# Top-64 attention kernel: diagonals of reciprocals for the turned probabilities, the test for missed rows on GpSimd, and VectorE in ScalarE's place for the first value product of a step

## What is computed

```python
dots = jnp.concatenate([q @ mem_k.T, q @ k.T]) * scale       # 16 memory keys + 512 keys, 16 heads
dots = jnp.einsum('bhij,hk->bkij', dots, pre_proj)           # heads mixed
dots = jnp.where(causal, neg, dots)
vk   = lax.top_k(dots, 64)[0][..., -1:]                      # the 64th largest of each row
attn = softmax(jnp.where(dots < vk, neg, dots))
attn = jnp.einsum('bhij,hk->bkij', attn, post_proj)          # heads mixed again
out  = (attn @ v) @ Wo + bo
x = x + layernorm(out);  x = x + layernorm(ffn(layernorm(x)))
```

## Time and profile before

| | |
|---|---|
| median of 3 runs | 3364.86 us (3363.4 to 3366.53) |
| the profiled execution's own time | 3363.66 us |
| its span, first to last instruction | 3361.9 us |
| TensorE busy | 2675.5 us (80%) |
| VectorE busy | 2958.5 us (88%) |
| ScalarE busy | 2891.6 us (86%) |
| GpSimd busy | 1887.2 us (56%) |
| mean granted TensorE clock | 0.903 |

### The profile page before, as it was taken

How to read it: one execution, slowest core, us unless ns; L and a number is a source line. 1 busy time by engine, 2 the same in 40 slices (tenths; PEclk the granted TensorE clock), 3 DMA queues, 4 the chain that set the end, 5 groups by cost and what they waited for, 6 DMA issues and landing times. The chain is left out here.

```text
span 3361.9 us, 70684 instructions
## 1 busy us (share of the span) xinstructions
PE 2675.5 (80%) x13754; PEld 1771.9 (53%) x13754; DVE 2958.5 (88%) x12547; ACT 2891.6 (86%) x8666; POOL 1887.2 (56%) x3623
## 2 busy tenths in 40 slices
PE   7878888888877888888787867887788887888765
PEld 3455555555545555555555545555455555555543
DVE  4599999999989999999999989998999999998985
ACT  1699989898978989999898978989899898989972
POOL 3455566555655555566565546655565665555543
PEclk8989899898988998999999888989899899999977
DMA  1000000000000000000000000000000000000000
GB/s 44 7 2 2 5 8 5 9 2 5 8 5 9 2 9 5 5 9 5 8 2 11 2 5 8 3 11 2 5 8 5 9 2 11 2 5 9 2 8 4
DMA packets 31404, 22.66 MB, mean 7 GB/s; under 512 B 3201, under 2 KB 30338, under 8 KB 30722
## 3 DMA queue, kind: packets, MB, share of 16 engines
q1 hardware_dynamic: 30722, 16.03, 1.7%
HBM read 11.83 MB, written 4.19 MB: 5 GB/s over the span
## 5 line engine op out<-in xcount | busy, mean ns | idle before, releaser
L913 ACT ACTIVATE signs<-scores,state 128x528 int8<-128x528 f32 (+3 forms) x3072 | 1723.5, 574 | 74.7 <-DVE state L1146 74.2
L1347 POOL TENSOR_SCALAR probs<-probs,rinv 128x528 f32<-128x528 f32 (+3 forms) x1024 | 538.9, 545 | 1300.6 <-DVE rinv L1193 1300.6
L783 PE MATMUL t_bank<-ident,probs 128*128 128x128 f32 x2560 | 485.5, 334 | 601.9 <-POOL probs L1347 593.6
L1355 POOL TENSOR_TENSOR work<-scores,work 128x528 f32<-128x528 f32 (+3 forms) x1024 | 888.3, 900 | 11.6 <-DVE work L1073 11.6
L759 PE MATMUL s_bank<-xn,gT 128*128 128x512 f32 (+3 forms) x2048 | 761.8, 496 | 1.8 <-ACT gT L844 0.7
L783 PEld LDWEIGHTS t_bank<-ident,probs 128*128 128x128 f32 x2560 | 325.7, 164 | 708.6 <-issue 582.5
L770 PEld LDWEIGHTS y_bank<-u_all,probsT 128*128 128x128 f32 x5120 | 616.8, 194 | 109.4 <-issue 98.8
L770 PE MATMUL y_bank<-u_all,probsT 128*128 128x128 f32 x5120 | 625.4, 278 | 6.6 <-ACT probsT L924 6.5
L924 ACT COPY probsT<-t_bank 128x512 f32<-128x512 f32 (+1 forms) x768 | 400.5, 522 | 251.2 <-PE t_bank L783 247.6
L913 ACT ACTIVATION_READ_ACCUMULATOR signs<-scores,state 128x1 f32 x3072 | 614.7, 200 | 0.0
L1073 DVE TENSOR_SCALAR_CACHE_REDUCE work<-scores,state 128x528 f32<-128x528 f32 (+3 forms) x1024 | 531.1, 553 | 46.2 <-DVE state L1146 46.2
(11 more groups left out here) (156 smaller groups left out, 2984.0 us busy)
## 6 DMA issues: line engine op xcount, KB each, us to landing
xwork<-in_L_attn_x_dram SPq DMA_DIRECT2D x17, 256.0 KB, 2.8
xres<-in_L_attn_x_dram SPq DMA_DIRECT2D x16, 256.0 KB, 2.9
out_dram<-ybuf SPq DMA_DIRECT2D x16, 256.0 KB, 2.4
u_all<-in_L_attn_Wq_dram SPq DMA_DIRECT2D x1, 512.0 KB, 3.5
u_all<-in_L_attn_Wk_dram SPq DMA_DIRECT2D x1, 512.0 KB, 4.4
u_all<-in_L_attn_Wv_dram SPq DMA_DIRECT2D x1, 512.0 KB, 5.3
u_all<-in_L_attn_Wo_dram SPq DMA_DIRECT2D x1, 512.0 KB
expo<-in_L_ffn_w_gate_dram SPq DMA_DIRECT2D x1, 192.0 KB, 4.7
```

The costliest lines, as they stand in the source:

```text
L783: mm = nc.tensor.transpose(t_bank[q % 2][:, at:at + P], probs[:, h % 2, KEY_AT[t] + j * P:KEY_AT[t] + (j + 1) * P], ident[:, :])
L913: nc.scalar.activation(signs[:, k, AT[t]:AT[t] + ROW[t]], row(scores, ring(head_of(s, k + 1), RING), t), ACT.Sign, bias=guesses(s % STATES ...
L1347: nc.gpsimd.tensor_scalar(prb, prb, rinv[:, slot_p, t:t + 1], 1.0, ALU.mult, ALU.mult).then_inc(scaled, 1)
L1355: nc.gpsimd.tensor_tensor(wrk, row(scores, slot_k, t), wrk, ALU.subtract).then_inc(hidden, 1)
```

## The change

It has three parts.

1. **Diagonals.** GpSimd no longer scales `probs` in place. It makes four 128 x 128 tiles `diag[t] = ident * rinv[t]`, and TensorE replaces each transpose by an ordinary matmul with the diagonal as its right side, which turns and scales at once. `pmem` is then a product with `rinv` and no longer a copy. Ahead of the diagonals GpSimd also waits for `t_full`, the last turn of the head before.
2. **Missed rows and `between` on GpSimd.** `spread` and `missed` leave VectorE; GpSimd makes them behind `offset`, which gets two more columns per tile (`reach`) so that `spread` is a product of two of them. The sum over the tiles is taken where VectorE copies the flags. The first operation of the secant step, `between = ...`, leaves VectorE too and stands behind `missed` on GpSimd; VectorE waits for it (`between_ready`) ahead of the operation that uses it.
3. **First value product.** The `U` product at place 0 of a step (nine of 16 steps: s = 0, 1, 2, 3, 4, 5, 9, 10, 15) is copied out of PSUM by VectorE, at the end of its step, and no longer by ScalarE.

```diff
@@ TensorE, turn
-                        mm = nc.tensor.transpose(t_bank[q % 2][:, at:at + P],
-                                                 probs[:, h % 2, KEY_AT[t] + j * P:KEY_AT[t] + (j + 1) * P], ident[:, :])
+                        mm = nc.tensor.matmul(t_bank[q % 2][:, at:at + P],
+                                              lhsT=probs[:, h % 2, KEY_AT[t] + j * P:KEY_AT[t] + (j + 1) * P],
+                                              rhs=diag[:, t, :], start=True, stop=True, skip_group_check=True)
@@ ScalarE, take_extra
-                            take_values(kind, b, par, use[1])
+                            if place == 1:
+                                take_values(kind, b, par, use[1])
@@ VectorE, step
-                        v.tensor_copy(flags[:, :], flag_part).then_inc(flag_taken, 1)
+                        v.tensor_scalar(flags[:, 0:T], flag_part, 1.0, None, ALU.mult, ALU.add,
+                                        accum_out=flags[:, T:T + 1]).then_inc(flag_taken, 1)
...
-                    if checks:
-                        number = found[:, (s - 1) % 2, :]
-                        dve.wait_ge(found_ready, 4 * ge + 4)
-                        alone(dve)
-                        v.scalar_tensor_tensor(out=spread[:, :], in0=number, scalar=-2.0 * AIM, in1=number,
-                                               op0=ALU.add, op1=ALU.mult).then_inc(select_step, 1)
-                        dve.wait_ge(select_step, 1)
-                        at_least(dve, flag_full, ge)
-                        alone(dve)
-                        v.scalar_tensor_tensor(out=missed[:, 0:T], in0=spread[:, :], scalar=WINDOW ** 2 + 0.5 - AIM ** 2,
-                                               in1=active, op0=ALU.is_gt, op1=ALU.mult,
-                                               accum_out=missed[:, T:T + 1]).then_inc(bad_ready, 1)
...
-                        v.tensor_tensor(between[:, :, :], pair(past, S_T, -1), pair(last, S_OTHER, 0),
-                                        ALU.subtract).then_inc(guess_step, 1)
...
-                        dve.wait_ge(guess_step, 3)
+                        dve.wait_ge(guess_step, 2)
+                        dve.wait_ge(between_ready, g - 1)
+                        alone(dve)
                         v.scalar_tensor_tensor(out=between[:, :, :],
...
+                    use = extra(kind, s, 0)
+                    if use is not None and use[0] == "U":
+                        u = use[1]
+                        dve.wait_ge(misc_full, misc_index(kind, b, use) + 1)
+                        at_least(dve, pv_done, (b - 1) * H + 4 * (u // 4) + 4)
+                        alone(dve)
+                        v.tensor_copy(u_all[:, u % 4, 512 * (u // 4):512 * (u // 4 + 1)],
+                                      misc[misc_place(kind, par, use)][:, :]).then_inc(misc_free[misc_place(kind, par, use)], 1)
@@ GpSimd, step
-                        nc.gpsimd.tensor_tensor(offset[:, :, 0:9], ranks,
-                                                found[:, (s - 1) % 2, :].unsqueeze(2).to_broadcast([P, T, 9]),
+                        nc.gpsimd.tensor_tensor(offset[:, :, 0:11], ranks,
+                                                found[:, (s - 1) % 2, :].unsqueeze(2).to_broadcast([P, T, 11]),
                                                 ALU.add).then_inc(offset_ready, 1)
+                        ge = g - LAG_E
+                        pool.wait_ge(offset_ready, ge + 1)
+                        alone(pool)
+                        nc.gpsimd.tensor_tensor(spread[:, :], offset[:, :, 0:1].squeeze(2), offset[:, :, 1:2].squeeze(2),
+                                                ALU.mult).then_inc(spread_ready, 1)
+                        pool.wait_ge(spread_ready, ge + 1)
+                        at_least(pool, flag_full, ge)
+                        alone(pool)
+                        nc.gpsimd.tensor_scalar(missed[:, :], spread[:, :], 0.0, 1.0, ALU.is_gt, ALU.mult).then_inc(bad_ready, 1)
+                    if any(lagged(kind, s, k + 2) for k in range(GUESSES)):
+                        last, past = (s - 1) % STATES, (s - 2) % STATES
+                        at_least(pool, guess_ready, g - 2)
+                        at_least(pool, first_ready, g - 1 if lagged(kind, s, 2) else 0)
+                        alone(pool)
+                        nc.gpsimd.tensor_tensor(between[:, :, :], pair(past, S_T, -1), pair(last, S_OTHER, 0),
+                                                ALU.subtract).then_inc(between_ready, 1)
                     extras(kind, b, s)
...
                         at_least(pool, probs_ready, 4 * gp + 4)
+                        at_least(pool, t_full, 3 * gp)
                         alone(pool)
                         for t in SCORE_ORDER:
-                            prb = probs[:, slot_p, AT[t]:AT[t] + ROW[t]]
-                            nc.gpsimd.tensor_scalar(prb, prb, rinv[:, slot_p, t:t + 1], 1.0, ALU.mult,
+                            nc.gpsimd.tensor_scalar(diag[:, t, :], ident[:, :], rinv[:, slot_p, t:t + 1], 1.0, ALU.mult,
                                                     ALU.mult).then_inc(scaled, 1)
```

More of the change, by code:

```diff
@@ L324, in build @@
         centre = sb("centre", [P, P])
+        diag = sb("diag", [P, T, P])
         row_sum = sb("row_sum", [P, 2 * HC])
@@ L342, in build @@
         found = sb("found", [P, 2, T])
-        offset = sb("offset", [P, T, 10])
+        offset = sb("offset", [P, T, 12])
         spread = sb("spread", [P, T])
-        missed = sb("missed", [P, T + 1])
+        missed = sb("missed", [P, T])
         flags = sb("flags", [1, T + 1])
@@ L443, in build @@
         select_step = sem("select_step")
+        spread_ready = sem("spread_ready")
         bad_ready = sem("bad_ready")
+        between_ready = sem("between_ready")
         scaled = sem("scaled")
@@ L1053, in _ @@
             dve.wait_ge(state_set, 3)
-            nc.vector.tensor_copy(offset[:, :, 9:10].squeeze(2), cap)
+            nc.vector.tensor_copy(offset[:, :, 11:12].squeeze(2), cap)
             def batch(kind, b, par):
@@ L1088, in step @@
                         dve.wait_ge(offset_ready, gp + 1)
[L1089 to L1090 removed]
+                        dve.wait_ge(select_step, T)
+                        v.scalar_tensor_tensor(out=offset[:, :, 2:11], in0=offset[:, :, 2:11], scalar=0.0,
                                                in1=candidates(past), op0=ALU.is_equal,
                                                op1=ALU.mult).then_inc(select_step, 1)
[L1093 removed]
+                        dve.wait_ge(select_step, T + 1)
                         dve.sem_clear(select_step)
[L1095 removed]
+                        v.tensor_reduce(kth[:, bass.ds(slot_p, 1), :].squeeze(1), offset[:, :, 2:12], AX_X,
                                         ALU.add).then_inc(kth_ready, 1)
[L1098 to L1109 removed]
                     if moves:
@@ L1358, in step @@
                             pool.wait_ge(misc_full, misc_index(kind, b, ("PM", 1)) + 1)
-                        pool.wait_ge(scaled, 4 * gp + 4)
                         alone(pool)
-                        nc.gpsimd.tensor_copy(head_mem(pmem, head_of(s, LAG_P)), mem_parts(probs[:, slot_p, :])).then_inc(pmem_ready, 1)
+                        shares = rinv[:, slot_p, :].rearrange("p (a t) -> p a t", a=2).unsqueeze(3)
+                        nc.gpsimd.tensor_tensor(head_mem(pmem, head_of(s, LAG_P)).rearrange("p a t m -> p a t m"),
+                                                mem_parts(probs[:, slot_p, :]), shares.to_broadcast([P, 2, 2, M]),
+                                                ALU.mult).then_inc(pmem_ready, 1)
                 def extras(kind, b, s):
```

32 lines of the change are left out of this document (15 added, 17 removed).

## The result

The changed kernel takes 3559.61 us (median of four runs, 3558.16 to 3561.91), the kernel before 3364.19: a ratio of 1.058 (95% interval 1.0562 to 1.0599), 195 us slower. The forecast was 255 slower. The page of its profiled execution has a span of 3556.8 us, where the earlier trace rows had 3361.9.

A forecast was written before the change was run, and what follows sets the result against it. VectorE was taken to set the pace, ScalarE close behind. Later use of `between`, 15.94 us a batch, 255 us in 16, added to 3363.66 gave 3619 us, 7.6% slower; range 3540 to 3695.

The forecast's parts named there:

- The mechanism: At L1123 VectorE would wait for GpSimd's `between`, queued behind `offset`, `spread` and `missed`: some 300 us in 256 steps.
- TensorE not the bound: Ten products for ten transposes add 1.1 us a step, hidden; the rival that TensorE becomes the bound: 3770, chance 0.04.
- What stands in front of the use of `between`: Delay of VectorE's use of `between`, summed by kind of step: +0.74 to +1.39 us, 15.94 us a batch.
- The chain from `offset` to the use: GpSimd's `offset`, `spread`, `missed`, `between` until VectorE's use: 1.42 us, bounds 1.15 to 1.7.
- steps with statistics: Steps s = 8, 9, 15 (+0.74 us) and, with a copy too, s = 1, 11 (+1.39), where `kth` comes later.
- What follows the use is unchanged: In VectorE's step behind its use of `between`, nothing changes, so the delay of the use is the step's.
- The relief of VectorE wins: Rival: VectorE's lighter load makes the kernel faster, full price -75 us, 3289; chance 0.03.
- The relief of ScalarE buys nothing: ScalarE also waits for the later guess, so 9/16 of a copy less a step gains nothing.

The follow-up runs named there:

- `between_on_vector`: The changed kernel with the `between` subtraction back on VectorE and its wait removed, all else kept; 3311.24 us, ratio 0.9829 to the kernel before.
- `only_copy`: The kernel before with only the first value product of a step copied out of PSUM by VectorE; 3443.89 us, ratio 1.0249.
- `copy_on_scalar`: The changed kernel with all value products copied by ScalarE again, `between` still last on GpSimd; 3547.88 us, ratio 1.0542 to the kernel before.
- `three_copies_norm`: The changed kernel with `between` on VectorE, one-source layer norms on GpSimd, and VectorE copying only in s = 1, 3, 5; 3247.71 us, ratio 0.966.
- `only_diag`: The kernel before with only the diagonals, products in place of transposes, and `pmem` with its own scaling; 3321.37 us, ratio 0.988.
- `one_source_norm`: The kernel before with GpSimd's layer norms made of one-source operations, a tile at a time; 3351.36 us, ratio 0.9968.
- `only_missed`: The kernel before with only the wider `offset`, `spread` and `missed` on GpSimd and the flags' sum in their copy; 3294.73 us, ratio 0.98.

## Why the prediction was right, and where its sizes were off

**The mechanism** held. The wait stands at L1123 with 309.0 us (forecast 300, bounds 200 to 400), GpSimd's wait for `rinv` is 5.2 us a step, and `between_on_vector` takes the whole loss away by undoing that one part. The diagonals take 374 ns (372), `pmem` starts 0.6 earlier behind `rinv`, `offset` starts at 5.96 to 5.99 where nothing delays it (5.97), the copy takes 0.68 (0.65), and `t_bank` has 5120 records, with TensorE not the bound. The Trainium skill, page "TensorE: Matmul & The Clock Gate", section Terms, has a transpose 4x faster for FP32. The trace does not agree. This is the row of the turns in the page of the kernel before, and the changed kernel's stands above:

```profile
L783 PE MATMUL t_bank<-ident,probs 128*128 128x128 f32 x2560 | 485.5, 334 | 601.9 <-POOL probs L1347 593.6
```

  2560 records of transposes became 5120 of products, and their busy time went from 485.5 to 831.5 us, a factor of 1.7, or 1.35 us a step, where the rows' factor of two gave 1.1 and the page's four 3.3. TensorE as a whole is busy 0.9 us a step more, at a granted clock of 0.921 for 0.903.

**The size** was 59 us too large. Three terms account for it; they sum to 61 us, and behind the last `rinv` the changed kernel takes 2 us more than the one before.

- *What stands in front of the use of `between`*, 34 us. The forecast had 15.94 us a batch, the means over the rows of both traces give 13.84. The chain from `offset` to the use takes 1.33 to 1.39, not 1.42: the gaps between `missed`, `between` and VectorE were taken a little long. In steps with statistics the use comes 0.2 to 0.45 earlier than summed, since `kth` starts at 6.21, and not at 6.39, and with a copy as well at 6.66 and 6.87, and not at 7.04. Why it does so was not tried. These two are 24 us. The other 10 lie in the kernel before, for which I took the use at 6.44 and 7.43 from two steps: in every second batch it comes at 6.7 to 6.9 in s = 0, 2, 12 and 14, and in s = 8 at 7.78 on average.
- *"What follows the use is unchanged"*, 21 us. This is the step of the prediction that failed. It holds in plain steps (4.90 to 4.93) but not in those with a norm. Before, L1146 took 0.95 in them; now it takes 0.17 in all, 46 us less in sum, because the guess comes at another time against GpSimd's norm. VectorE's and GpSimd's timelines in step s = 9 of the changed kernel:

```profile
1439.06 0.18 DVE L1188 RECIPROCAL rinv<-rowsum 128x4 f32<-128x4 f32 x1
...
1448.29 0.17 DVE L1141 TENSOR_TENSOR state<-state,move 128x12 f32<-128x12 f32 x1
...
1448.62 0.76 DVE L1081 TENSOR_SCALAR_CACHE_REDUCE work<-scores,state 128x528 f32<-128x528 f32 x1 [0.17 <-DVE state L1141]
...
1451.94 0.18 DVE L1188 RECIPROCAL rinv<-rowsum 128x4 f32<-128x4 f32 x1
...
1448.56 1.04 POOL L1272 TENSOR_TENSOR xwork<-xres,rstd 128x512 f32<-128x512 f32 x1
```

  The step takes 12.88, less than the 13.14 of before, in a kernel that is 195 us slower. The product that held L1146 now starts at 1448.56, behind it, and the one-source count L1081 runs beside it undisturbed. In s = 1, 8 and 15 the hold comes anew, on the products of probabilities. VectorE and GpSimd in s = 15 of the changed kernel:

```profile
1529.25 1.18 DVE L1183 SCALAR_TENSOR_TENSOR probs<-scores,kth,expo 128x528 f32<-128x528 f32 x1
...
1530.36 1.08 DVE L1183 SCALAR_TENSOR_TENSOR probs<-scores,kth,expo 128x400 f32<-128x400 f32 x1
...
1529.14 0.73 POOL L1278 TENSOR_TENSOR ybuf<-xres,ybuf 128x256 f32<-128x256 f32 x1
1529.82 1.19 POOL L1279 TENSOR_TENSOR ybuf<-xres,ybuf 128x256 f32<-128x256 f32 x1
```

  The two products take 0.77 and 0.63 where GpSimd is idle. The sum over a batch is 1.30 in favour of the changed kernel, most of it (0.74) from s = 9.
- *The way to the first `rinv`*, 6 us shorter (151.5 for 157.7 us). It comes with the copy: 151.0 in `only_copy`, 156.2 in `copy_on_scalar`, and 154.5 to 157.8 in the other kernels without a copy in every place. The other kernels with it have 150.6 to 153.4. How it comes about was not followed up.

**The rivals.** "The relief of VectorE wins" had its price right in kind: with `between` in time the kernel is 54 us faster (forecast 75). Its condition was not met, as said. "The relief of ScalarE buys nothing" held in the changed kernel, but not in the faster ones: there ScalarE is late in part of the steps, and the best kernel, `three_copies_norm`, shares the copies between the two engines.

## What to carry to other kernels

Before an operation goes to an idle engine, read where in the step that idle time lies and what stands ahead in its queue. The operation here takes 0.17 us, and it cost 248 us behind three others, and still 28 when its result was early, since it had filled a gap between two dependent operations and the wait for it is not free. Measure the parts of a change together with their neighbours: four parts that sum to +48 made +195. Leaving out the one that moved `between`, and most of the copies, took the loss away and left a gain. And when two engines read the same memory side by side, look at what a longer or shorter operation of the one falls on: a hold that went from one operation came back on others behind it in three of four steps.

## What the runs showed of the hardware

- **VectorE's two-source operations and GpSimd's operations hold each other, and on GpSimd's side one source is enough.** A VectorE product of 12 elements takes 0.95 in place of 0.17 us under GpSimd's two-source product of 512 columns (1.04 us) and 0.30 under the first of four one-source ones of 128 columns (0.37 us each); in both it ends when GpSimd's operation does (1572.07 and 1572.04; 1369.12 and 1369.10). The other way, GpSimd's sum of 256 columns takes 1.16 in place of 0.73 beside VectorE's two-source products, and a one-source tile up to 0.87 in place of 0.37. VectorE's one-source count of 528 columns is never held: 0.77 at most in 256 of them, in each of the traces before, after, `one_source_norm` and `three_copies_norm`. The Trainium skill, page "SBUF — State Buffer", section "SBUF: two separate sides", has the shared pair of ports as an exclusive lock, held for a whole instruction, and names a VectorE operation with two SBUF inputs against a GpSimd operation that reads SBUF. These rows agree with it.
- **Two operations of GpSimd held little or nothing.** Its power of 4 elements (`rstd`, 1.04 us) ran beside VectorE's two-source operations of 12 and 24 elements without making them longer: L1136 of the kernel before takes 0.18 in 59 steps in which it starts with 0.77 us of `rstd` left. And beside the tile with two scalars (below) L1146 took 0.19 with 0.72 us of it left. Here the rows differ from the page's "whole instruction", and the measurement decides; no run shows why.
- **A subtraction and a product with two scalars per row took twice a product with one.** In `one_source_norm` the norm with a mean and a reciprocal per row takes 0.79 to 0.80 us a tile of 128 columns where nothing holds it (931 ns on average with the held ones), the one with a reciprocal alone 373 to 375 ns. Whether it is the second scalar or the subtraction was not taken apart.
- **The granted clock was higher where TensorE had more to do in the time.** It was 0.90 in the kernel before, 0.92 in the changed one, and 0.945 to 0.96 in `only_diag`, `between_on_vector` and `three_copies_norm`, all with 16314 products; `only_missed` with 13754 has 0.91. These are means over the span of the two levels, 1.2 and 2.4 GHz. What the clock was worth in time was not tried in any of them.
